# Sparse expert layer: who multiplies silu by the routing weight, and from where

## The reference

```python
gates = softmax(xt @ Wg.T); scores, inds = top_k(gates, 2); scores /= sum(scores)
g = einsum('td,ehd->teh', xt, We_gate);  u = einsum('td,ehd->teh', xt, We_up)
h = silu(g) * u                              # 16 experts, 64 hidden each
y_all = einsum('teh,edh->ted', h, We_down)
y = sum(take(y_all, inds) * scores)          # the two chosen experts
shared = silu(xt @ Ws_gate.T) * (xt @ Ws_up.T) @ Ws_down.T
y = y + sigmoid(xt @ Wsg.T) * shared
x = x + tanh(g_ffn[1]) * y
```

## Time and profile before

| what | us |
|---|---|
| median of 3 runs | 180.69 (180.67 to 180.72) |
| span of the profiled execution, first to last instruction | 178.9 |
| TensorE busy in the span | 165.0 (92%) |
| VectorE busy | 126.0 (70%) |
| ScalarE busy | 83.7 (47%) |
| GpSimd busy | 54.7 (31%) |

### The profile page before, as it was taken

How to read it: one execution, slowest core, us unless ns; L and a number is a source line. 1 busy time by engine, 2 the same in 40 slices (tenths; PEclk the granted TensorE clock), 3 DMA queues, 4 the chain that set the end, 5 groups by cost and what they waited for, 6 DMA issues and landing times.

```text
span 178.9 us, 3936 instructions
## 1 busy us (share of the span) xinstructions
PE 165.0 (92%) x1530; PEld 105.9 (59%) x1538; DVE 126.0 (70%) x341; ACT 83.7 (47%) x154; POOL 54.7 (31%) x91
## 2 busy tenths in 40 slices
PE   7998999999999998888597799999999998999993
PEld 5644546665455454466365676647577665666672
DVE  0579365779779879698988698659838494654453
ACT  2255775654664655768566951365230313212210
POOL 8635652267884723436023005200002000000000
PEclk9999999999999999999999999999999999999999
DMA  5986000000000000000000000000000000100001
GB/s 157 395 297 286 0 0 5 4 2 4 2 4 4 0 4 0 0 4 2 0 4 0 0 0 4 0 2 0 2 4 0 0 0 0 59 4 0 0 0 59
DMA packets 1890, 5.83 MB, mean 33 GB/s; under 512 B 208, under 2 KB 592, under 8 KB 1744
## 3 DMA queue, kind: packets, MB, share of 16 engines
q1 hardware_dynamic: 1152, 4.01, 6.2%
q10 hardware_dynamic: 720, 1.57, 2.4%
HBM read 5.06 MB, written 0.52 MB: 31 GB/s over the span
## 4 chain that ended last, share of the span: by engine, by line
PE 68%; DVE 16%; ACT 7%; POOL 4%; issue 3%; POOLq 0%; DVEq 0%
PE banks L1342 10%; PE banks L1367 10%; PE banks L1345 10%; PE banks L1132 8%; DVE banks L748 4%; PE banks L1124 3%; PE banks L1178 3%; PE banks L1181 2%; POOL vz L264 2%; ACT ffn_work L536 2%; PE banks L1355 2%; ACT f_hqT L542 2%; PE banks L1162 2%; PE banks L1036 2%; PE banks L1152 2%
## 5 line engine op out<-in xcount | busy, mean ns | idle before, releaser
L748 DVE TENSOR_REDUCE banks<-banks 128x8 f32<-128x1024 f32 x16 | 19.7, 1230 | 10.8 <-PE banks L1132 10.8
L302 POOL TENSOR_SCALAR_AFFINE_SELECT pT<-pT 128x512 f32<-128x512 f32 x32 | 19.9, 644 | 24.2 <-ACT pT L459 24.1
L1367 PEld LDWEIGHTS banks<-ews,rest 128*128 128x128 f32 x160 | 20.6, 191 | 7.8 <-issue 7.7
L1036 PE MATMUL banks<-idle 128*128 128x256 bf16 x158 | 23.0, 293 | 1.2 <-DVE idle L659 1.2
L636 ACT ACTIVATE full<-banks 128x512 f32<-128x512 f32 x20 | 11.9, 593 | 21.9 <-PE banks L1342 21.9
L459 ACT ACTIVATE pT<-banks 128x512 f32<-128x512 f32 x32 | 17.3, 594 | 8.7 <-PE banks L1162 8.6
L1367 PE MATMUL banks<-ews,rest 128*128 128x128 f32 x160 | 21.0, 275 | 0.0
L1342 PE MATMUL banks<-nT,ews 128*128 128x512 f32 x40 | 20.6, 597 | 0.2
L994 DVE TENSOR_TENSOR xnT<-full,banks 128x512 f32<-128x512 f32 x20 | 13.7, 683 | 9.6 <-PE banks L1345 7.3
L1345 PE MATMUL banks<-nT,ews 128*128 128x512 f32 x40 | 20.4, 592 | 0.0
L1036 PEld LDWEIGHTS banks<-idle 128*128 128x128 bf16 x158 | 16.4, 105 | 5.2 <-DVE idle L659 1.2
(11 more groups left out here) (170 smaller groups left out, 287.7 us busy)
## 6 DMA issues: line engine op xcount, KB each, us to landing
ews<-in_ew SPq DMA_DIRECT2D x1, 1928.5 KB, 7.3
fws<-in_fw SPq DMA_DIRECT2D x1, 768.0 KB, 8.1
cT<-in_ctxT ACTq DMA_DIRECT2D x2, 256.0 KB, 5.3
x_all<-in_x SPq DMA_DIRECT2D x2, 256.0 KB, 4.7
lws<-in_lw ACTq DMA_DIRECT2D x1, 449.0 KB, 8.4
sels<-in_sel ACTq DMA_DIRECT2D x1, 320.0 KB, 8.7
a<-in_aw ACTq DMA_DIRECT2D x1, 256.0 KB, 5.1
out_x<-x_all SPq DMA_DIRECT2D x1, 256.0 KB, 2.0
```

What stands on the lines that cost most here:

```text
L302: nc.gpsimd.affine_select(out=probs, in_=probs, compare_op=ALU.is_ge, fill=0.0, base=0, pattern=[[0, HG], [1, S]], channel_multiplier=-1). ...
L748: V.tensor_reduce(bank[2 * p][:, 0:2 * HG], banks[p][:, :].rearrange("p (h k) -> p h k", h=2 * HG), AX.X, ALU.max).then_inc(sm["a_mx"], 1)
L1036: mm(bank[t][:, 0:2 * S], idle[:, 0:128], idle[:, :], start=True, stop=True)
L1367: last = mm(bank[t][:, b * D:(b + 1) * D], e_h[:, u, b * S:(b + 1) * S], expert(c)[2], start=(c == 0 and (b == 0 or s == 1 and b == 2)), s ...
```

## The change

Chunks 0 and 1 stay as they are. From chunk 2 on the three factors are multiplied in another order and by other engines: ScalarE copies the spread weights from PSUM into a new SBUF tile `e_g` (`spread_copy`), GpSimd multiplies `e_sil` by them into `e_t` (`gate_weighted`), and VectorE multiplies `e_t` by up, read from PSUM, into `e_h`. The waits follow: TensorE's up(k+2) waits for `e_h` of chunk k, where it waited for `e_t`; a spread waits for the copy that empties its bank. `rstd_of(3, 1)` moves behind GpSimd's product for chunk 4, and `spread_copy(k)` stands at the end of ScalarE's step k, behind that step's side job.

```diff
+        e_g = sb("e_g", [128, 2, W])
...
-            for s in range(2):
-                rstd_of(2, s)
-                bias_into_x(s)
-                rstd_of(3, s)
+            def gate_weighted(k):
+
+                m, u = spread_of(k), k % 2
+                pool.wait_ge(sm["e_silr"], k + 1)
+                pool.wait_ge(sm["e_gs"], m - 1)
+                pool.wait_ge(sm["e_hr"], k - 1)
+                nc.gpsimd.tensor_tensor(e_t[:, u, :], e_sil[:, u, :], e_g[:, m % 2, :], ALU.mult)\
+                    .then_inc(sm["e_tr"], 1)
+
+            rstd_of(2, 0)
+            bias_into_x(0)
+            rstd_of(3, 0)
+            rstd_of(2, 1)
+            bias_into_x(1)
+            for k in range(2, 2 * NC):
+                gate_weighted(k)
+                if k == 4:
+                    rstd_of(3, 1)
...
+            def spread_copy(k):
+
+                m = spread_of(k)
+                if k % NC == NC - 1:
+                    return
+                act.wait_ge(sm["e_Gp"], m + 1)
+                if m >= 4:
+                    act.wait_ge(sm["e_tr"], max(j for j in range(k) if spread_of(j) == m - 2) + 1)
+                nc.scalar.activation(e_g[:, m % 2, :], bank[4 + m % 2][:, :], ACT.Copy).then_inc(sm["e_gs"], 1)
+
             for k in range(2 * NC):
                 act.wait_ge(sm["e_gp"], k + 1)
                 if k >= 2:
...
                 elif k == 9:
                     wT_copy(1)
+                if k > 1:
+                    spread_copy(k)
...
             def gate_times_up(k):
-                u = k % 2
                 dve.wait_ge(sm["e_silr"], k + 1)
                 dve.wait_ge(sm["e_up"], k + 1)
-                V.tensor_tensor(e_t[:, u, :], e_sil[:, u, :], bank[2 + u][:, :], ALU.mult).then_inc(sm["e_tr"], 1)
-
+                V.tensor_tensor(e_t[:, k, :], e_sil[:, k, :], bank[2 + k][:, :], ALU.mult).then_inc(sm["e_tr"], 1)
+
+            gate_times_up(0)
+            gate_times_up(1)
             for k in range(2 * NC):
                 u = k % 2
-                if k != 1:
-                    gate_times_up(k)
-                if k == 0:
-                    gate_times_up(1)
                 dve.wait_ge(sm["e_tr"], k + 1)
-                dve.wait_ge(sm["e_Gp"], spread_of(k) + 1)
-                if k >= 2:
+                if k < 2:
+                    dve.wait_ge(sm["e_Gp"], k + 1)
+                    other = bank[4 + k]
+                else:
+                    dve.wait_ge(sm["e_up"], k + 1)
                     dve.wait_ge(sm["e_yp"], k - 1)
-                V.tensor_tensor(e_h[:, u, :], e_t[:, u, :], bank[4 + spread_of(k) % 2][:, :],
-                                ALU.mult).then_inc(sm["e_hr"], 1)
+                    other = bank[2 + u]
+                V.tensor_tensor(e_h[:, u, :], e_t[:, u, :], other[:, :], ALU.mult).then_inc(sm["e_hr"], 1)
...
                 mm(bank[u][:, :], expert(c)[0], nT4[:, s, :], start=True, stop=True).then_inc(sm["e_gp"], 1)
-                if k >= 2:
+                if k >= 4:
+                    pe.wait_ge(sm["e_hr"], k - 1)
+                elif k >= 2:
                     pe.wait_ge(sm["e_tr"], k - 1)
                 mm(bank[2 + u][:, :], expert(c)[1], nT4[:, s, :], start=True, stop=True).then_inc(sm["e_up"], 1)
...
                 pe.wait_ge(sm["wTs"], s + 1)
-                if m >= 2:
-                    pe.wait_ge(sm["e_hr"], max(j for j in range(k) if spread_of(j) == m - 2) + 1)
+                if m >= 4:
+                    pe.wait_ge(sm["e_gs"], m - 3)
+                elif m >= 2:
+                    pe.wait_ge(sm["e_hr"], m - 1)
```

More of the change, by code:

```diff
@@ L182, in build @@
             n4r t4p t4s lgp lgs r_top r_both r_two r_rest r_chosen r_le r_th r_wt r_split wTp wTs
-            e_Gp e_gp e_up e_silr e_tr e_hr e_yp e_y2 e_res""".split()
+            e_Gp e_gs e_gp e_up e_silr e_tr e_hr e_yp e_y2 e_res""".split()
         sm = {n: sem(n) for n in names}
```

## The result

The changed kernel takes 192.4 us, the median of four runs (191.36 to 194.23), against 180.69 before: 1.0657 times as long, with an interval of 1.06 to 1.0713. The profiled execution is the longest of the four: 194.23 us, with a span of 192.5. The four differ by more than the kernel before ever did, and TensorE's mean granted clock differs with them: 0.990, 0.991, 0.980 and 0.971 in runs of 191.36, 191.99, 192.81 and 194.23 us. So there are two things to find: some 10 us that every run has, and 0.6 to 3.5 us that go with the clock.

A forecast was written before the change was run, and what follows sets the result against it. TensorE bounds the kernel, instruction behind instruction; seven stops from the longer path to `e_h` add 10.15 us to the 178.9 us span, giving 189.1, plus 1.79 to the median run: 190.8 us, range 186.7 to 195.5.

The forecast's parts named there:

- up(4): TensorE's up-projection of chunk 4, waiting on chunk 2, whose copy stands behind `exp3(1)`: a stop of 0.33 us.
- up(6): Up-projection of chunk 6, waiting on chunk 4, whose copy stands behind `pT3_copy(1)`: a stop of 0.56 us.
- up(7): Up-projection of chunk 7, waiting on chunk 5, whose GpSimd product stands behind `rstd_of(3,1)`: a stop of 2.68 us.
- up(8): Up-projection of chunk 8, waiting on chunk 6, whose copy stands behind `xT4_copy(1)`: a stop of 2.41 us.
- up(9): Up-projection of chunk 9, waiting on chunk 7, whose copy stands behind `logits_copy(1)` and `shared_tanh(1)`: a stop of 2.29 us.
- up(10): Up-projection of chunk 10, waiting on chunk 8, whose copy stands behind `chosen_tanh(1)`: a stop of 1.11 us.
- end: Last chunks: GpSimd's products 18 and 19 run back to back, so down(19) starts late: 0.77 us.
- The tail: End of ScalarE's copy to TensorE's go, through GpSimd's product, VectorE's product and hand-overs: 2.20 us.
- Steady chunks: Chunks 10 to 17: new path of 2.83 us under 3.68 us of TensorE work, cover 0.85 us, costing nothing.
- the clock: Rival, 10%: idle in the stops drops TensorE to 1.2 GHz; one piece gives 193 us, all 199.5.
- Every chunk behaves like the steady ones: Rival, 4%: only the end's 0.77 us is lost, 181.5 us; with a product under 0.88 us, 180.7.
- The table load comes first: Rival, 6%: silu(3)'s table load of 1.28 us comes ahead of copy(2), lengthening the stop at chunk 2: 192.1 us.

The follow-up runs named there:

- the kernel with the filled stops: Changed kernel with 18, 14, 14 and 5 idle matmuls, results unused, ahead of up(7), up(8), up(9), up(10): 190.74 us, ratio 1.0555.
- the longer chunks: The kernel with both orders, plus a second, unused GpSimd product ahead of each of products 11 to 17: 184.84 us, ratio 1.0226.
- the kernel with both orders: Changed kernel with ScalarE's copies ahead of each step's side job and GpSimd's last rstd behind its product 5: 182.78 us, ratio 1.0116.
- the orders mended: The kernel with both orders, plus product 6 behind VectorE's normalizations, copy 2 behind `exp3(1)`, chunks 18 and 19 multiplied on VectorE: 181.54 us, ratio 1.0043.
- the rstd moved: Changed kernel with GpSimd's last rstd behind its product 5 instead of ahead of it, copies left behind the side jobs: 188.81 us, ratio 1.046.
- a single stop of 1.66 us: Changed kernel with each ScalarE copy ahead of its step's side job instead of behind it: 184.31 us, ratio 1.0198.

## Why the prediction was right, and where its size was off

**The mechanism and the sum held.** The forecast was 190.8 us with the clock left as it was; with the stops filled and the clock at 1.00 the changed kernel takes 190.74. Stop by stop, from the kernel with the filled stops: the start of the up less the start due (0.86 after its gate, which is where the fillers begin), and 0.10 because an up after a wait takes 1.12 us, where the prediction reckoned with the 1.02 that an up without a wait has in these rows. The end is taken from the 24 matmuls of down(17) to down(19), from 182.53 to 183.79 + 2.39; in the timeline of the kernel before they stand without a gap:

```profile
173.03 3.09 PE L1367 MATMUL banks<-ews,rest 128*128 128x128 f32 x24
```

| stop before | predicted us | measured us |
|---|---|---|
| up(4) | 0.33 | 0.29 + 0.10 = 0.39 |
| up(6) | 0.56 | 0.53 + 0.10 = 0.63 |
| up(7) | 2.68 | 139.57 - 137.12 + 0.10 = 2.55 |
| up(8) | 2.41 | 145.32 - 142.94 + 0.10 = 2.48 |
| up(9) | 2.29 | 151.30 - 149.06 + 0.10 = 2.34 |
| up(10) | 1.11 | 154.97 - 154.01 + 0.10 = 1.06 |
| end | 0.77 | 186.18 - 182.53 - 3.09 = 0.56 |

That makes 10.0 us of the 10.1 by which the span grew (189.0 - 178.9). No stop is off by more than 0.21 us, but that the sum is right to 0.1 us is in part luck: the restart costs 0.10 more at each up, and up(7) and the end are shorter than forecast. The tail, from the end of a copy to TensorE's go, was taken as 2.20 and measures 2.17 before up(8) (144.55 to 146.72), with 0.13 us from ScalarE to GpSimd where 0.07 was taken, and 0.03 from GpSimd to VectorE where 0.11 was.

**The product.** 1.267 us, as the bias sum had it. The estimate of 1.11 us from the 2.6 cycles per element in the Trainium skill's GPSIMD Engine Reference, section 3.1, is too low here. The advice of its section 4.1 against GpSimd for such work is borne out as to speed, 1.27 us against 0.69. But the speed costs time only where the chain is late: moving the products back to VectorE with the same orders left 5.2 of 10.1 us (185.9), moving copy and rstd with the products on GpSimd left 2.1.

**Steady chunks** lost nothing, as forecast, but the cover is smaller than the 0.85 us that was worked out: 1.24 us more per chunk made the ups 0.52 us late, so 0.72 us were covered. The prediction let ScalarE's copy start 0.24 us after the start of the spread (0.21 + 0.03); in the kernel after it starts 0.41 us after it (164.34 to 164.75). That the longer chunks came out at 184.84 us, near the 185.0 expected, is in part luck too: each stop was longer, and the one at the end was covered.

**The step that was mis-sized is the clock.** It was a rival with a chance of 10%, at 193 for one piece or 199.5 for all, and the sum carried nothing for it; a falling clock was among the prediction's own signs of being wrong, and there it was wrong. In fact the clock was below 1.00 in all four runs, and they took 0.6 to 3.5 us more than 190.74, median 1.7. It and the forecast were not alternatives: the stops came as predicted, and the clock came on top. The argument against it, that matmuls of 1.9 to 2.8 us stand between the stops, failed: they did not hold the clock up, the fillers did. What the clock takes varies from run to run for the same kernel, from 0.971 to 0.991. That brief idling between groups makes the clock swing is what the Trainium skill's page TensorE: Matmul & The Clock Gate says in "A second HAM failure mode: psum-queue depth-cycling", and this trace agrees: three falls to 0.50 and three returns between 140.4 and 157.5 us, around stops of 1.95 to 2.28 us.

**The other rivals.** "Every chunk behaves like the steady ones" didn't happen in the changed kernel, but the kernel with both orders comes near the 181.5 us that it names, at 182.78. "The table load comes first" didn't happen: the load of silu's table stands behind copy 2 in the kernel after, as priced. The load that did cost time, in the kernel with both orders, was the exponential's, which the prediction had not looked at because it was hidden.

## What to carry to other kernels

Here TensorE was the bound, and fewer products on VectorE gained nothing: 18 fewer made the kernel slower, and 16 fewer with the orders mended still took 181.54 us against 180.7. A new link in the chain cost time only where its place in a queue made it late: for each instruction added, ask what stands ahead of it in its engine's list and what that waits for. A copy behind a job that waits for the bounding engine turns a queue into a loop, and whatever part of its latency that engine has no other work for is paid each time. Price TensorE's idle twice, once as time and once as the clock that may fall after it.

## What the runs showed of the hardware that was not expected

A product on GpSimd that reads SBUF holds up some of VectorE's instructions: four normalizations (tensor_scalar, 128x128) took 2.07 us beside it and 1.12 alone, a 128x64 comparison of two SBUF tiles 1.11 and 0.23 (this product was not moved; the 0.23 are from kernels without a product beside it). VectorE's product of an SBUF and a PSUM tile stayed at 0.69. The prediction had looked only at whether VectorE makes GpSimd's product longer, not at the reverse. The Trainium skill has this in SBUF — State Buffer, section "Who interferes with whom": VectorE and GpSimd share a port pair that one of them holds for a whole instruction, and an instruction with one SBUF input outside the two-port modes stays clear of it. The sizes above agree with it; no run shows the ports themselves.

TensorE's clock fell without any idle time of more than 2.3 us. In the changed kernel's profile it was full up to the end of the stop of 2.28 us and fell 0.8 us later, fell again 0.5 us after the stop of 1.95 us, and a third time 0.2 us before the stop of 2.07 us ended; with the rstd moved it stayed full after the stop of 2.22 us and fell at the end of the next, of 2.08; with a single stop of 1.66 us it stayed full. What decides whether it falls these runs leave open. The same program had mean clocks from 0.971 to 0.991 in four executions, and 2.9 us between its times.
